# Row weights of a routed expert layer picked by GpSimd, row statistics and last normalisations two pairs a tile, additions to the result two by two

## The chip, the cores and the metric

The kernel runs on one core of one Trainium2 chip. The metric is the device time of one execution in microseconds; lower is better.

## The reference

For 2 x 1024 tokens of width 256 the result is `x + attention(xn) + experts(xn)`, with `xn` the rows of `x` normalised to mean 0 and variance 1.

```
xn = layernorm(x)
# "attention": a gated recurrence in logarithms
k = xn @ W_z.T + b_z
log_values = [g_log(h0) ; -softplus(-k) + g_log(xn @ W_h.T + b_h)]
a_star = pad(cumsum(-softplus(k), axis=-1))
log_h = a_star + cumlogsumexp(log_values - a_star, axis=1)
log_h = (log_h - log_h.mean()) / std(log_h)           # over everything
y = exp(log_h)[:, 1:, :] + xn
attention = layernorm(y) * ln_w + ln_b                # row by row
# experts: 8 experts, top 2 of each token, inner width 704
for e in range(8):
    experts += (silu(xn @ w1[e].T) * (xn @ w3[e].T)) @ w2[e].T * weight_of(e)
```

## The kernel before

**Setup.** The rows are normalised into `xn` (part of `xrow`, which holds for each token its 256 values and its two routing weights), transposed, and routed. The 4096 picks are sorted by expert into tiles of 128 rows, an expert's rows filling whole tiles; there are at least 33 tiles (`SURE`) and at most 39 (`NTILES`), and this input makes 36, numbered 0 to 35. `xrow` is stored to `xn_dram`, from which GpSimd gathers the rows of a tile with an indirect DMA (L390) into one of `DEEP` = 4 buffers `xg`.

**The tile loop.** It runs on all engines at once, each in its own fixed order, with semaphores between them. For tile j:

- TensorE: `up(j)` (L1296, 18 products: float32 values are split into a high and a low part, three products for one), the transpose of the rows of tile j+1 (L1265), a few instructions of the attention (`between`), `down(j-1)` (L1314, 18 products), and the transpose of the gated values, `h_tile(j)` (L1326).
- ScalarE: `silu(j)` (L595), the high part of the next rows (L572), `y_copy(j-1)` (L621: the down product times the row weights `wrow`, into a buffer of four, `ysb`), the high part of `hT` (L590), then its share of the next expert's weights (L604). In some tiles one attention step stands before or behind these, between two loads of an activation table (L696, L704).
- VectorE: `gate(j)` (L961), the low part of the next rows, `x_lo` (L952), `slot_weight(j+1)` (L1067: the weight of each of the 128 rows, one element a partition), `between(j)`, the low part of `hT`, `h_lo(j)` (L956), `after(j)`.
- GpSimd: `gather(j+4)` (L390), `scatter(j-1)` (L406: an indirect DMA that adds a tile's rows to the result), and `split_due(j)` (L424: the low parts of the next expert's weights, `raw` minus the high part).

**Weights.** Each expert's weights go through four pieces. While the first tile of an expert is at work two pieces of the next one are due, with its second tile one, with its third one. ScalarE makes a piece's high part, GpSimd its low part. `up` of an expert's first tile waits for three of its pieces, `down` for all four (`s_w`). The 28 pieces of L424 are those of experts 1 to 7, and on this input experts begin with tiles 0, 4, 9, 13, 18, 23, 28 and 32.

**Attention.** Its steps are put by hand into `between` and `after` of tiles 1 to 32: running maxima (tiles 3 to 9), scans (10 to 12), sums and statistics over all elements (13 to 18), the exponential (ScalarE, 19 and 20), then, for pairs m = 0 to 7 of 128-row blocks, `h_back(m)` on TensorE (L1354, four transposes) and `row_stats(m)` on VectorE in tile 20 + m, the square roots on ScalarE in tiles 24 and 28, `row_scales` in 25 and 29, and `last_norm(m)` (L1054, L1059) behind `h_lo` in tile 25 + m.

**Additions to the result.** `out` starts as a copy of x. Additions to it must not overlap, so each `scatter` waits until the one before has landed (`rows_added`: `s_st`), and until the attention's parts so far have landed (`s_ab`). `add_attention` (L413) adds a quarter of the attention rows, 512 KB, by a DMA from GpSimd's queue, with the same wait, before tiles 27, 29 and 31 and behind tile 32. Behind the loop come the tiles from 33 on, each in a nested condition (`tail`), then the last down product and a last scatter (L467) from `hst`.

Of the kernel before, what the change touches and what calls it, by code (L numbers as in the profile page):

```python
# [14 lines left out]
P = 128  # L15
B, T, D = 2, 1024, 256
# [36 lines left out]
def build_program(nc, x, small, w_main, w_tail, out, xn_dram):  # L53
# [5 lines left out]
    with ctx:  # L59
# [285 lines left out]
        def _(pool):  # L345
# [38 lines left out]
            def gather(j):  # L384

                if j >= DEEP:
# [4 lines left out]
                                        bass.IndirectOffsetOnAxis(gidx[:, j:j + 1], 0)).then_inc(s_gt[k], 16)  # L391

            def rows_added(j, parts):

                if j:
                    pool.wait_ge(s_st, 16 * j)
                if j == 0:
                    pool.wait_ge(s_fill, 16)
                if parts:
                    pool.wait_ge(s_ab, 16 * parts)  # L400
# [7 lines left out]

            def add_attention(j, m):

                pool.wait_ge(s_p2, 4 * m + 4)
                rows_added(j, m)
                pool.dma_start(out[4 * m * P:4 * (m + 1) * P, :].rearrange("(t p) d -> p t d", p=P),  # L413
                               xn[:, 4 * m:4 * m + 4, :], accum_op=ALU.add).then_inc(s_ab, 16)

# [10 lines left out]

            for j in range(DEEP + 1):
                gather(j)
            pool.wait_ge(s_idx, 1)
            pool.wait_ge(s_ctl, 1)  # L430
            split_due(0, 0)

            def tile(i, u, done=None, parts=PARTS_OF_H):

                j = LOOP * i + (1 + u)
                if j + DEEP < NTILES:
                    gather(j + DEEP)
                scatter(j - 1, parts)
                if done is None:
                    done = pool.value_load(plan[0:1, ds(j, 1)], min_val=0, max_val=PIECES * (E - 1))  # L440
                return split_due(done, j)

            added = 0
            for i in range(8):
                done = pool.value_load(plan[0:1, ds(LOOP * i + 1, 1)], min_val=0, max_val=PIECES * (E - 1))
                for u in range(LOOP):
                    j = LOOP * i + 1 + u
                    if j in (27, 29, 31):
                        add_attention(j - 1, added)
                        added += 1  # L450
                    done = tile(i, u, done, added)
            add_attention(SURE - 1, added)

# [20 lines left out]
        def _(act):  # L474
# [170 lines left out]

            def row_deviations(h):
                act.wait_ge(s_p1, 3 * (4 * h + 4))
                act.activation(std[:, 8 * h:8 * h + 8], mv[:, 8 * h:8 * h + 8, 1], ACT.Sqrt,
                               bias=eps[:, :]).then_inc(s_std3, 1)

# [32 lines left out]
            def roots(j):  # L683
                if j == 18:
                    deviation()
                else:
                    row_deviations((j - 24) // 4)

# [20 lines left out]
            for i in range(8):  # L709
                done = act.value_load(plan[0:1, ds(LOOP * i + 1, 1)], min_val=0, max_val=PIECES * (E - 1))  # L710
                for u in range(LOOP):
                    j = LOOP * i + 1 + u
                    if j in (3, 4, 5, 6, 7, 10, 11, 12, 13, 19, 20):
                        done = tile(i, u, done, "natural_log_exp_and_others", exp_log_first, exp_log_second)
                    elif j in (18, 24, 28):
                        done = tile(i, u, done, "sqrt_and_others", None, roots)
                    else:
                        done = tile(i, u, done)
# [11 lines left out]
        def _(dve):  # L730
# [315 lines left out]

            def row_scales(h):
                dve.wait_ge(s_std3, h + 1)
                dve.reciprocal(rstd[:, 8 * h:8 * h + 8], std[:, 8 * h:8 * h + 8]).then_inc(s_rs3, 1)
                dve.wait_ge(s_rs3, h + 1)  # L1050

# [10 lines left out]

            def slot_weight(j):

                k = j % DEEP
                dve.wait_ge(s_gt[k], 16 * (j // DEEP + 1))
                dve.scalar_tensor_tensor(wrow[:, j:j + 1], xg[:, k, D:D + 1], first_pick[:, j:j + 1],  # L1067
                                         xg[:, k, D + 1:D + 2], ALU.mult, ALU.max).then_inc(s_ws, 1)

            softplus(0)  # L1070
# [5 lines left out]
            x_lo(0, 0, xT0_ps)  # L1076
            slot_weight(0)
            softplus(2)
            add_cumsum(1)
            x_lo(1, 1, xT1_ps)  # L1080
            slot_weight(1)
            dve.wait_ge(s_u0b, 2)
# [10 lines left out]
            def between(j):  # L1093
# [12 lines left out]
                if 13 <= j <= 16:  # L1106
                    plus_max(j - 13)
                if 20 <= j <= 27:
                    row_stats(j - 20)

            def after(j):
# [32 lines left out]
                if j == 18:  # L1144
                    normaliser()
                if j in (25, 29):
                    row_scales((j - 25) // 4)
                if 25 <= j <= 32:
                    last_norm(j - 25)

            def tile(i, u, hooks=False):
# [3 lines left out]
                if not isinstance(j, int) or j < NTILES - 1:  # L1155
                    x_lo(j + 1, u % 2)
                    slot_weight(j + 1)
                if hooks:
# [12 lines left out]
        def _(pe):  # L1171
# [185 lines left out]
            def between(j):  # L1357
                if j in (4, 5, 6, 7):
                    half_cumsum(j // 2, 1 - j % 2)
                if 20 <= j <= 27:  # L1360
                    h_back(j - 20)

# [6 lines left out]
            def tile(i, u, hooks=False):  # L1369
# [12 lines left out]
                pe.reg_mov(r_e, expert(j + 1))  # L1382
                h_tile(j)

            for i in range(8):
# [45 lines left out]
```

## Time and profile before

| | |
|---|---|
| Median of 3 runs | 357.61 us (355.52 to 359.3) |
| The profiled execution's own time | 357.79 us |
| Its span, first to last instruction | 356.1 us |
| Mean granted TensorE clock, share of full speed | 0.969 |
| PE, DVE, ACT, POOL busy | 325.8, 260.8, 219.9, 206.4 us |

What lies outside the span is 1.7 us. Busy shares are means over stages with different limits: what a change is worth is read tile by tile. The names are PE for TensorE, DVE for VectorE, ACT for ScalarE, POOL for GpSimd. A GpSimd instruction's recorded start and end are rough.

### The profile page before, as it was taken

What the parts mean: (1) busy time and instruction counts of PE and PEld (TensorE: products, weight loads), DVE (VectorE), ACT (ScalarE), POOL (GpSimd) and SP (SyncE); (2) the same over time, 40 slices, a digit from 0 to 9 for tenths busy, and PEclk for the clock granted to TensorE, in tenths of its full rate; (3) what the DMA queues carried; (4) which work ended last, traced back from release to release, by engine and by line L of the source; (5) the groups of instructions that cost most, each with busy time, mean ns of one, the idle gap of its engine ahead of it and who ended that gap; (6) DMA issues with size and microseconds to landing.
All of it is one profiled execution on the core that took longest, in us unless ns stands there. A gap on an engine that the chain in (4) does not pass through costs nothing.

```text
span 356.1 us, 6682 instructions
## 1 busy us (share of the span) xinstructions
PE 325.8 (91%) x1964; PEld 273.9 (77%) x1964; DVE 260.8 (73%) x466; ACT 219.9 (62%) x328; POOL 206.4 (58%) x137
## 2 busy tenths in 40 slices
PE   8998999799999999999898999999999999979830
PEld 8883464588878898997787899889898988969730
DVE  5488787989996899889899842584589668763300
ACT  2547997455879974999854269934853485323400
POOL 4500023159968674989899728563885475945331
PEclk9999969989999999999999999999999999999985
DMA  7924912005444542354354434542463534354621
GB/s 263 426 120 137 293 52 59 15 11 150 122 82 115 142 101 32 80 129 129 44 144 109 102 38 115 142 101 33 84 181 89 75 45 76 47 76 49 98 38 15
DMA packets 19086, 37.00 MB, mean 104 GB/s; under 512 B 2272, under 2 KB 13536, under 8 KB 19008
## 3 DMA queue, kind: packets, MB, share of 16 engines
q0 software_dynamic: 9168, 11.97, 21.5%
q1 hardware_dynamic: 8496, 22.56, 20.4%
q10 hardware_dynamic: 1376, 1.85, 1.4%
q8 instruction: 29, 0.48, 0.6%
q14 instruction: 17, 0.14, 0.1%
HBM read 27.45 MB, written 11.03 MB: 108 GB/s over the span
## 4 chain that ended last, share of the span: by engine, by line
PE 54%; DVE 23%; ACT 8%; issue 8%; DMA 2%; ACTq 1%; POOL 1%; POOLq 0%; DVEq 0%
PE PS L1296 23%; PE PS L1314 11%; PE PS L1190 6%; PE PS L1326 5%; DVE wrow L1067 3%; DVE tmp L961 3%; PE PS L1176 2%; DMA out<-work,sidx 2%; DVE hT L956 2%; DVE U L985 2%; DVE A L998 1%; PE PS L1220 1%; DVE xrow L1054 1%; DVE xrow L1059 1%; PE PS L1265 1%
## 5 line engine op out<-in xcount | busy, mean ns | idle before, releaser
L1296 PE MATMUL PS<-wbuf,xT 128*128 128x512 f32 (+1 forms) x648 | 149.6, 384 | 4.9 <-issue 3.7
L1296 PEld LDWEIGHTS PS<-wbuf,xT 128*128 128x128 f32 x648 | 118.3, 190 | 29.4 <-issue 9.3
L424 POOL TENSOR_TENSOR wbuf<-raw,wbuf x28 | 81.4, 2924 | 23.1 <-ACT wbuf L604 21.4
L406 POOL DMA_INDIRECT out<-work,sidx x35 | 62.7, 1792 | 53.2 <-ACT work L621 20.1
L1314 PE MATMUL PS<-wbuf,hT 128*128 128x256 f32 x648 | 86.8, 288 | 0.0
L1314 PEld LDWEIGHTS PS<-wbuf,hT 128*128 128x128 f32 x648 | 79.3, 189 | 1.9 <-issue 1.9
L390 POOL DMA_INDIRECT work<-xn_dram,gidx x39 | 50.4, 1292 | 51.8 <-DVE gidx L892 36.1
L595 ACT ACTIVATE tmp<-PS 128x512 f32<-128x512 f32 x72 | 32.0, 460 | 41.6 <-PE PS L1296 41.3
L961 DVE TENSOR_TENSOR tmp<-tmp,PS 128x512 f32<-128x512 f32 x72 | 35.0, 516 | 29.4 <-ACT tmp L595 28.6
L956 DVE TENSOR_TENSOR hT<-PS,hT 128x768 fp32r<-128x768 f32 x36 | 34.2, 949 | 29.3 <-ACT hT L590 24.2
L621 ACT ACTIVATE work<-PS,wrow 128x256 f32<-128x256 f32 x35 | 16.4, 470 | 38.0 <-PE PS L1314 38.0
L1067 DVE SCALAR_TENSOR_TENSOR wrow<-work,first_pick 128x1 f32<-128x1 f32 x37 | 37.1, 1003 | 0.0
L1326 PE MATMUL PS<-ident,tmp 128*128 128x128 f32 x216 | 30.1, 275 | 5.7 <-DVE tmp L961 5.6
L590 ACT ACTIVATE hT<-PS 128x768 fp32r<-128x768 f32 x35 | 28.4, 810 | 10.4 <-PE PS L1326 10.4
L1190 PE MATMUL PS<-xnT_M,small_sb 128*128 128x512 f32 x64 | 32.3, 646 | 1.0 <-ACT tmp L525 1.0
L604 ACT ACTIVATE wbuf<-raw x28 | 30.4, 1110 | 4.0 <-issue 3.9
L1326 PEld LDWEIGHTS PS<-ident,tmp 128*128 128x128 f32 x216 | 24.0, 141 | 7.9 <-DVE tmp L961 6.9
L1190 PEld LDWEIGHTS PS<-xnT_M,small_sb 128*128 128x128 f32 x64 | 12.6, 208 | 14.1 <-issue 12.9
L704 ACT ACT_TABLE_LOAD x14 | 18.0, 1283 | 0.3
L696 ACT ACT_TABLE_LOAD x14 | 18.0, 1283 | 0.3
L952 DVE TENSOR_TENSOR xT<-PS,xT 128x256 fp32r<-128x256 f32 x37 | 15.5, 419 | 0.1
L572 ACT ACTIVATE xT<-PS 128x256 fp32r<-128x256 f32 x37 | 14.0, 381 | 1.7 <-PE PS L1265 1.7
(185 smaller groups left out, 350.7 us busy)
## 6 DMA issues: line engine op xcount, KB each, us to landing
raw<-w_main SPq DMA_DIRECT2D x24, 544.0 KB
raw<-w_main SPq DMA_DIRECT2D x8, 416.0 KB
xn_dram<-xrow SPq DMA_DIRECT2D x4, 516.0 KB, 7.2
out<-xrow POOLq DMA_DIRECT2D x4, 512.0 KB, 6.1
xrow<-x SPq DMA_DIRECT2D x4, 256.0 KB, 4.8
xrow<-x ACTq DMA_DIRECT2D x4, 256.0 KB, 5.4
small_sb<-small ACTq DMA_DIRECT2D x1, 768.0 KB, 7.9
work<-xn_dram,gidx POOLq DMA_INDIRECT x39
```

The source lines that it names most:

```text
L390: pool.indirect_dma_start(xg[:, k, :], None, xn_dram, bass.IndirectOffsetOnAxis(gidx[:, j:j + 1], 0)).then_inc(s_gt[k], 16)
L406: pool.indirect_dma_start(out, bass.IndirectOffsetOnAxis(sidx[:, j:j + 1], 0), ysb[:, j % DEEP, :], None, compute_op=ALU.add).then_inc(s_s ...
L424: pool.tensor_tensor(lo, raw[:, ds(part, WP)], hi.bitcast(fp32), ALU.subtract).then_inc(s_w, 1)
L595: act.activation(sls[n], w1_ps[n], ACT.Silu).then_inc(s_silu, 1)
L604: act.activation(wslot(p // PIECES + 1, 0, part), raw[:, ds(part, WP)], ACT.Copy).then_inc(s_hi, 1)
L956: dve.tensor_tensor(hT[:, 1, :], hT_ps, hT[:, 0, :].bitcast(fp32), ALU.subtract).then_inc(s_hlo, 1)
L961: dve.tensor_tensor(g_hs[n], sls[n], w3_ps[n], ALU.mult).then_inc(s_g, 1)
L1067: dve.scalar_tensor_tensor(wrow[:, j:j + 1], xg[:, k, D:D + 1], first_pick[:, j:j + 1], xg[:, k, D + 1:D + 2], ALU.mult, ALU.max).then_inc ...
L1190: ins = pe.matmul(PS[:, base + qo * CH:base + (qo + 1) * CH], wzh_sb[:, q, mat, qo * P:(qo + 1) * P], xnT[:, q, c * CH:(c + 1) * CH], star ...
L1296: ins = pe.matmul(PS[:, at:at + cols], xT[:, slot, xpart, q * P:(q + 1) * P], wbuf[:, w, wpart, q * 2 * F + at:q * 2 * F + at + cols], sta ...
L1314: ins = pe.matmul(y_ps, hT[:, hpart, c * P:(c + 1) * P], wbuf[:, w, wpart, W13 + c * D:W13 + (c + 1) * D], start=(c == 0 and hpart == 0 an ...
L1326: ins = pe.transpose(hT_ps[:, c * P:(c + 1) * P], g_h[:, a:a + P], ident[:, :])
```

## The change

Four things are moved, and no arithmetic is altered:

1. `slot_weight(j)` leaves VectorE for GpSimd, which makes it two tiles ahead: at the head of its tile j it does `slot_weight(j+2)`. There it is a `tensor_scalar` with two pointer scalars.
2. Row statistics: `h_back` and `row_stats` run two pairs a tile in tiles 20 to 23, where they ran one pair a tile in tiles 20 to 27. On TensorE the second `h_back` stands behind `h_tile(j)`.
3. `last_norm` runs two pairs a tile in tiles 25 to 28 (one before `h_lo`, one behind), where it ran one a tile in tiles 25 to 32. The square roots of all rows are made once, in tile 24, so that tile 28 loads no table.
4. `add_attention` adds two quarters in one go, before tiles 28 and 30.

In the order of the diff: GpSimd (to the second `add_attention`), ScalarE (`row_deviations` and its tiles), VectorE (`between`, `after`, `tile`), TensorE (`between`, `tile`).

```diff
+            def slot_weight(j):
+                k = j % DEEP
+                pool.wait_ge(s_gt[k], 16 * (j // DEEP + 1))
+                pool.tensor_scalar(wrow[:, j:j + 1], xg[:, k, D:D + 1], first_pick[:, j:j + 1],
+                                   xg[:, k, D + 1:D + 2], ALU.mult, ALU.max).then_inc(s_ws, 1)
...
-            def add_attention(j, m):
-                pool.wait_ge(s_p2, 4 * m + 4)
-                rows_added(j, m)
-                pool.dma_start(out[4 * m * P:4 * (m + 1) * P, :].rearrange("(t p) d -> p t d", p=P),
-                               xn[:, 4 * m:4 * m + 4, :], accum_op=ALU.add).then_inc(s_ab, 16)
+            def add_attention(j, first):
+                pool.wait_ge(s_p2, 4 * first + 8)
+                rows_added(j, first)
+                for m in (first, first + 1):
+                    pool.dma_start(out[4 * m * P:4 * (m + 1) * P, :].rearrange("(t p) d -> p t d", p=P),
+                                   xn[:, 4 * m:4 * m + 4, :], accum_op=ALU.add).then_inc(s_ab, 16)
...
-            for j in range(DEEP + 1):
+            for j in range(DEEP):
                 gather(j)
             pool.wait_ge(s_idx, 1)
+            slot_weight(0)
+            gather(DEEP)
+            slot_weight(1)
+            slot_weight(2)
...
                 j = LOOP * i + (1 + u)
+                if j + 2 < NTILES:
+                    slot_weight(j + 2)
                 if j + DEEP < NTILES:
                     gather(j + DEEP)
                 scatter(j - 1, parts)
...
-                    if j in (27, 29, 31):
+                    if j in (28, 30):
                         add_attention(j - 1, added)
-                        added += 1
+                        added += 2
                     done = tile(i, u, done, added)
-            add_attention(SURE - 1, added)
...
-            def row_deviations(h):
-                act.wait_ge(s_p1, 3 * (4 * h + 4))
+            def row_deviations():
+                act.wait_ge(s_p1, 3 * NT // 2)
...
-                    elif j in (18, 24, 28):
+                    elif j in (18, 24):
...
-                if 20 <= j <= 27:
-                    row_stats(j - 20)
+                if 20 <= j <= 23:
+                    row_stats(2 * (j - 20))
+                if j == 25:
+                    row_scales()
+                if 25 <= j <= 28:
+                    last_norm(2 * (j - 25))
...
-                if j in (25, 29):
-                    row_scales((j - 25) // 4)
-                if 25 <= j <= 32:
-                    last_norm(j - 25)
+                if 20 <= j <= 23:
+                    row_stats(2 * (j - 20) + 1)
+                if 25 <= j <= 28:
+                    last_norm(2 * (j - 25) + 1)
...
                     x_lo(j + 1, u % 2)
-                    slot_weight(j + 1)
...
-                if 20 <= j <= 27:
-                    h_back(j - 20)
+                if 20 <= j <= 23:
+                    h_back(2 * (j - 20))
...
                 h_tile(j)
+                if hooks and 20 <= j <= 23:
+                    h_back(2 * (j - 20) + 1)
```

## Rows read from the trace of the kernel before

**Rows 1.** The page, parts 1 and 4: busy time; the shares of the chain.
```profile
PE 325.8 (91%) x1964; PEld 273.9 (77%) x1964; DVE 260.8 (73%) x466; ACT 219.9 (62%) x328; POOL 206.4 (58%) x137
...
PE 54%; DVE 23%; ACT 8%; issue 8%; DMA 2%; ACTq 1%; POOL 1%; POOLq 0%; DVEq 0%
PE PS L1296 23%; PE PS L1314 11%; PE PS L1190 6%; PE PS L1326 5%; DVE wrow L1067 3%; DVE tmp L961 3%; PE PS L1176 2%; DMA out<-work,sidx 2%; DVE hT L956 2%; DVE U L985 2%; DVE A L998 1%; PE PS L1220 1%; DVE xrow L1054 1%; DVE xrow L1059 1%; PE PS L1265 1%
```

**Rows 2.** Lines L1067 and L424: ns min/median/max, first and last start.
```profile
L1067 DVE SCALAR_TENSOR_TENSOR wrow<-work,first_pick x37: 202/475/3761, 62.9 to 334.7; 128x1 f32<-128x1 f32 x37
...
L424 POOL TENSOR_TENSOR wbuf<-raw,wbuf x28: 2502/2750/4583, 75.1 to 308.1; - x28
```

**Rows 3.** Timeline of VectorE, tiles 3 and 32: start, duration, instruction.
```profile
92.72 2.95 DVE L1067 SCALAR_TENSOR_TENSOR wrow<-work,first_pick 128x1 f32<-128x1 f32 x1
95.60 2.34 DVE L968 TENSOR_TENSOR_SCAN xnT_M<-U,u 128x1024 f32<-128x1024 f32 x1
...
308.15 3.75 DVE L1054 SCALAR_TENSOR_TENSOR xrow<-xrow,mv,small_sb 128x256 f32<-128x256 f32 x2
...
316.10 0.87 DVE L1054 SCALAR_TENSOR_TENSOR xrow<-xrow,mv,small_sb 128x256 f32<-128x256 f32 x2
```

**Rows 4.** Timeline of GpSimd, tile 3 and from tile 26 to the end.
```profile
92.55 3.10 POOL L424 TENSOR_TENSOR wbuf<-raw,wbuf  x1
...
270.98 1.58 POOL L406 DMA_INDIRECT out<-work,sidx  x1 [1.30 <-ACT work L621]
275.44 1.40 POOL L413 DMA_DIRECT2D out<-xrow  x1 [2.88 <-DMA out<-work,sidx]
...
282.49 1.66 POOL L406 DMA_INDIRECT out<-work,sidx  x1 [4.26 <-DMA out<-xrow]
...
302.44 3.12 POOL L424 TENSOR_TENSOR wbuf<-raw,wbuf  x1
...
308.10 3.12 POOL L424 TENSOR_TENSOR wbuf<-raw,wbuf  x1
...
347.79 1.57 POOL L467 DMA_INDIRECT out<-hst,scol  x1 [2.67 <-DMA out<-work,sidx]
```

**Rows 5.** Windows: length; busy PE, PEld, DVE, ACT, POOL; clock, DMA share, GB/s.
```profile
70.55:102.79 32.24, 31.67 (x180) 27.11 (x181) 30.46 (x36) 21.00 (x31) 25.95 (x11) 0.95 0.38 92
154.48:203.11 48.63, 44.14 (x267) 38.23 (x267) 46.33 (x53) 32.25 (x48) 43.58 (x21) 1.00 0.49 115
133.65:140.50 6.85, 6.85 (x47) 6.26 (x46) 6.85 (x10) 2.49 (x6) 2.74 (x2) 1.00 0.27 42
217.15:233.58 16.43, 15.54 (x98) 13.52 (x97) 8.07 (x15) 15.63 (x21) 11.82 (x7) 1.00 0.54 135
240.90:248.18 7.28, 7.28 (x51) 6.69 (x49) 4.07 (x10) 2.49 (x6) 2.58 (x2) 1.00 0.27 41
262.77:270.86 8.09, 7.76 (x51) 6.75 (x50) 7.95 (x16) 3.82 (x8) 5.88 (x4) 1.00 0.54 131
285.01:299.28 14.27, 14.22 (x92) 12.59 (x90) 11.18 (x19) 9.57 (x16) 9.64 (x6) 1.00 0.41 58
```

**Rows 6.** Timeline of TensorE: up products of tiles 32, 33, 35; last down product.
```profile
306.15 4.11 PE L1296 MATMUL PS<-wbuf,xT 128*128 128x512 f32 x18
...
315.85 4.10 PE L1296 MATMUL PS<-wbuf,xT 128*128 128x512 f32 x18 [1.50 <-issue]
...
329.58 4.09 PE L1296 MATMUL PS<-wbuf,xT 128*128 128x512 f32 x18
...
339.65 2.38 PE L1314 MATMUL PS<-wbuf,hT 128*128 128x256 f32 x18
```

**Rows 7.** Group of GpSimd with one element a partition: busy us, mean ns.
```profile
L461 POOL COPY scol<-sidx 128x1 uint32 x1 | 0.2, 183 | 0.4 <-issue 0.4
```

**Rows 8.** DMA of one attention add: us to landing; window in its middle.
```profile
DMA to landing us min/median/max: 5.9/6.1/6.3
...
279.00:281.00 2.00, 2.00 (x10) 1.63 (x9) 1.72 (x3) 0.25 (x1) 0.00 (x0) 1.00 1.19 202
```

More of the change, by code:

```diff
@@ L644, in normal_exp @@
                 act.activation(Ag[:, g, :], Ag[:, g, :], ACT.Exp, scale=gs[:, 8:9], bias=gs[:, 9:10]).then_inc(s_hx, 1)
-            def row_deviations(h):
-                act.wait_ge(s_p1, 3 * (4 * h + 4))
-                act.activation(std[:, 8 * h:8 * h + 8], mv[:, 8 * h:8 * h + 8, 1], ACT.Sqrt,
-                               bias=eps[:, :]).then_inc(s_std3, 1)
+            def row_deviations():
+                act.wait_ge(s_p1, 3 * NT // 2)
+                act.activation(std[:, :], mv[:, :, 1], ACT.Sqrt, bias=eps[:, :]).then_inc(s_std3, 1)
             def exp_log_first(j):
@@ L686, in roots @@
                 else:
-                    row_deviations((j - 24) // 4)
+                    row_deviations()
             def tile(i, u, done=None, table=None, first=None, second=None):
@@ L1045, in row_stats, with row_scales @@
                 ins.then_inc(s_p1, 1)
[L1047 to L1050, printed above, removed]
+            def row_scales():
+                dve.wait_ge(s_std3, 1)
+                dve.reciprocal(rstd[:, :], std[:, :]).then_inc(s_rs3, 1)
+                dve.wait_ge(s_rs3, 1)
             def last_norm(m):
@@ L1061, in last_norm @@
                 ins.then_inc(s_p2, 1)
[L1063 to L1068, printed above, removed]
             softplus(0)
@@ L1076, in _ @@
             x_lo(0, 0, xT0_ps)
-            slot_weight(0)
             softplus(2)
@@ L1080, in _ @@
             x_lo(1, 1, xT1_ps)
-            slot_weight(1)
             dve.wait_ge(s_u0b, 2)
```

## The prediction

> **What bounds the kernel now.** I read the page first, then windows tile by tile, then the timelines of the tiles that are longer than the rest. TensorE is busy 91% of the span and holds 54% of the chain that ended last; VectorE holds 23% [rows 1]. A tile in which nothing waits takes 6.86 us, as tile 9 does, from 133.65 [rows 5]. Against it three kinds are longer. In tiles 1 to 4 and 12 to 17 (from 70.55 and from 154.48) VectorE is busy 30.46 of 32.24 us and 46.33 of 48.63: it paces them. In tiles 20 and 21 (from 217.15) ScalarE does, 15.63 of 16.43 us, with table loads and exponentials. Tile 23 (240.90 to 248.18) carries one `h_back`, 7.28 for 6.86, so four transposes cost 0.43 us [rows 5]. Single tiles stand out: 26 (8.09 us) and 32 (9.70, from 306.15 to 315.85) [rows 5, 6]. And the end isn't TensorE's: its last down product ends at 342.03, but the last scatter starts at 347.79, because GpSimd's additions, each waiting until the one before has landed, are behind [rows 4, 6].
>
> **Part 1, row weights.** On VectorE one takes 202 ns at least, 475 in the median and up to 3761 [rows 2], and the chain puts 3% of the span, some 11 us, on L1067 [rows 1]. The timeline shows what the long ones are: the one at 92.72 ends at 95.67, and GpSimd's piece of weights runs from 92.55 to 95.65 [rows 3, 4]. An instruction with two inputs in SBUF waits for GpSimd's to end. Who takes the wait over when the row weight is gone? The next VectorE instruction with two inputs in SBUF. In tile 3 that is the scan at 95.60 (`U`, `U`), which would start at 92.7 into the same piece [rows 3, 4]; likewise `less_n` in tiles 1 and 2, the scans in 8 to 10 and 12, `plus_max` in 13 to 16. In the other tiles the next step reads PSUM (4 to 7, 11, 20 to 27), but there VectorE doesn't pace. So the long waits are worth 0; only the undisturbed instruction is saved. Of its 0.20 us some 0.07 overlaps its neighbour (the scan starts at 95.60, the row weight ends at 95.67 [rows 3]), which leaves 0.13. Ten paced tiles and two in the setup: 12 x 0.13 = 1.6 us gained. The bounds are 0 and the chain's 11.
>
> The Trainium skill, "SBUF — State Buffer", section "Who interferes with whom", says that a VectorE instruction with two SBUF inputs and a GpSimd one that reads SBUF exclude each other, and whoever issues first has the pair for the whole instruction. The trace agrees in tile 3. By that rule the order decides, so that VectorE, 0.13 us earlier, could now win where it lost: rival 1.
>
> On GpSimd the new instruction has no row. The nearest is the copy of one element a partition, 0.18 us with 0.4 idle before it [rows 7]; the far bound is one kept waiting by a VectorE scan, 2.34 us [rows 3]. I take 0.3, near the copy. Queued behind it are `gather`, `scatter` and `split_due`, and TensorE and ScalarE wait for those. But GpSimd is busy 58% [rows 1], and the weight is used two tiles later: it costs nothing until tile 27, and after that one of them lies on GpSimd's chain (part 4). The waits of 2.34 belong to tiles up to 12.
>
> **Part 2, statistics.** `h_back` costs 0.43 us where TensorE paces. Tiles 20 and 21 are ScalarE's: 16.43 us against 2 x 7.28 leave 1.9 us of waiting, in which their second ones hide. Tiles 22 and 23 gain one (+0.86), tiles 24, 25 and 27 lose theirs (-1.29); in 26 VectorE's wait for a piece of weights fills what comes free. Sum -0.4. VectorE has room for a second `row_stats`: it is busy 4.07 of 7.28 us in tile 23 [rows 5], one of them included.
>
> **Part 3, last normalisations.** An undisturbed pair of instructions takes 0.87 us, so a `last_norm` 1.75 [rows 3]. Two of them beside some 2.4 us of the usual work (tile 23's 4.07 less its statistics, about 1.7) make 5.9 of 6.86: tiles 25 to 28 hold. In tile 32 a pair takes 3.75 us, because the piece from 308.10 to 311.22 runs [rows 3, 4], and the tile becomes 9.70 us, 2.84 too long. Of that 1.5 stands as "issue" before `up(33)` [rows 6], where the nested tail begins, and stays; 1.3 goes, as no normalisation is left in tile 32. So does 0.55 in tiles 29 and 30 (14.27 us from 285.01 [rows 5]), which is ScalarE behind a table load and VectorE behind a piece. Sum -1.9.
>
> **Part 4, additions, and what hangs on them.** Let S be the start of `up(27)`, 270.86 before, where tile 26's window ends [rows 5]. From one add of attention to the scatter behind it GpSimd needs 282.49 - 275.44 = 7.05 us, 6.1 of them to landing [rows 4, 8]. Two in a row have no row. In the middle of one, data flow at 202 GB/s [rows 8], so the second's 0.51 MB adds 2.6 us at least; if it is as slow as the first it adds 4.7 (6.1 less the issue, 1.40 [rows 4]). That is 8.7 to 10.8 to landing; I take the middle, 9.8, and 10.6 to the scatter.
>
> GpSimd's new course, TensorE taking 6.86 a tile: `scatter(26)` at S + 7.8; it has landed 4.46 later (270.98 to 275.44 [rows 4]); the first two adds at S + 12.3; `scatter(27)` at S + 22.9; after 1.4, two pieces of 2.6 (2502 ns at least, median 2750 [rows 2]) to S + 29.5; row weight, gather, `scatter(28)` at S + 31.2; 1.1 later expert 7's third piece, to S + 34.9. `up(32)`, the first of expert 7, is due at S + 5 x 6.86 = S + 34.3. Before, the piece ended at 305.56 and `up(32)` began at 306.15 [rows 4, 6]: 0.6 us to spare; now it is late, and with the start-up behind the wait TensorE loses 1.3. The second two adds go at S + 35.4, `scatter(29)` at S + 46.0, and the fourth piece ends at S + 49.8; before, it ended at 311.22 = S + 40.4 [rows 4]. `down(32)` is due at S + 35.6 + 6.86 + 1.5 + 4.1 = S + 48.1; TensorE loses 2.0. Two new waits, +3.3.
>
> The end: from the start of `up(35)`, 329.58 [rows 6], to the end of the span at 356.1 it is 26.5 us. No add of attention stands between scatters any more after S + 46; five scatters at 4.5 us bring `scatter(34)` to S + 68.5, and its rows, ready 7 us behind `up(35)` at S + 59.7, have hardly waited. The last row copy follows 12.6 us behind `up(35)` (its last down product ends 12.45 behind it [rows 6]), the last scatter 1.4 later, and the end 8.3 behind that (347.79 to 356.1 [rows 4]): 22.3 us, -4.2.
>
> **The sum**: -1.6 - 0.4 - 1.9 + 3.3 - 4.2 = -4.8. It is made against the profiled execution's own 357.79, of which 1.7 lies outside the span: 353.0. That execution stands 0.2 above the median of the runs shown, which I neglect.
>
> **Rivals.** (1) Row weights' waits are real gains, partly because VectorE now gets in first, and the weights of expert 7 are in time. For it: some 11 us of the chain [rows 1]. Against it: tile 3's next instruction. A quarter of them beyond my 1.6 gives -2.3, no new wait at tile 32 -3.3: 347.4. (2) Nothing to speak of: a pair of adds shares the queue with a gather and takes 2.4 more than I say. Each us of that counts twice for the fourth piece: +4.5, 357.5. (3) Slower: the second add gains nothing from the first, so that pair and gather take 2 x 7.05 + 1 = 15.1 to the scatter, 4.5 over mine. The fourth piece is 9 later, `down(32)` waits for it, 362.0. It turns slower than before when a pair takes more than 2.4 us over my 10.6. (4) The change doesn't do what it says, row weights on GpSimd coming late behind scans. With two tiles of lead it is next to nothing, and would look like rival 2.
>
> The Trainium skill, "GPSIMD Engine Reference", section "Performance versus the Vector engine", has GpSimd about twice as slow at elementwise work: an estimate from that page is 0.4 us for VectorE's 0.2. The one on the chain would cost 0.1 more, the sum 353.1; no run here shows it yet.
>
> **Chances.** Forecast 0.50, rival 1 0.22, rival 2 0.17, rival 3 0.08, rival 4 0.03. Within 1%, 3.6 us, is about what a measurement of this kernel can't tell from no change: 354.0 to 361.2. The forecast's own spread, 350 to 356 by the bounds of a pair and of the 1.6, puts a third of it there. Faster: 0.33 + 0.22 and a little = 0.57; same 0.36; slower 0.07. The range of 8 in 10 reaches from 346.5, just beyond rival 1, to 358.0, just beyond rival 2.
>
> **What would show it.** VectorE's instruction behind `x_lo` in tiles 3, 12 and 15 should be the long one now, up to 2.9 us over its usual time. Tiles 29 and 30 should take 6.86. The scatter behind a pair should start 10.6 us behind its first add. `up(32)` and `down(32)` should wait for L424. The last scatter should start within 1.5 us of the last row copy. I am wrong if those scans are short (rival 1), if a pair takes 13 us or more (rival 3), or if TensorE waits for statistics in tiles 22 to 25.

## The result and the profile after

The changed kernel takes 364.35 us in the median of four runs (363.06 to 366.3), the kernel before 356.89 beside it on the same chip (355.52 to 359.3). The ratio is 1.0193, with a 95% interval from 1.0139 to 1.0246: slower, by 1.4 to 2.5%, where 353.0 us and a gain of 4.8 were forecast, and beyond the range. The profiled execution took 365.17 us, with a span of 363.4 against 356.1; the changed parts are read from it.

From the page, part 1, then the GpSimd row of part 2 (busy tenths in 40 slices of 9.1 us), and two groups of part 5:

```profile
PE 331.9 (91%) x1964; PEld 278.9 (77%) x1964; DVE 252.3 (69%) x428; ACT 217.3 (60%) x325; POOL 237.8 (65%) x175
...
POOL 4500024169999999999899937864699346948731
...
L397 POOL TENSOR_SCALAR wrow<-work,first_pick 128x1 f32<-128x1 f32 x38 | 54.4, 1433 | 0.1
...
L997 DVE TENSOR_TENSOR_SCAN U<-tmp,U 128x1024 f32<-128x1024 f32 x4 | 15.7, 3918 | 0.0
```

VectorE has lost 8.5 us of busy time against [rows 1], GpSimd has gained 31.4. Its 65% is a mean: from about 80 to 210 us nearly every slice is 9 tenths full. The 38 row weights alone take 54.4 us on it. The view of their source line:

```profile
L397 POOL TENSOR_SCALAR wrow<-work,first_pick x38: 353/1002/3043, 57.7 to 345.8; 128x1 f32<-128x1 f32 x38
```

An undisturbed one takes 0.35 us, the median is 1.00 and the longest 3.04. On VectorE the three numbers were 0.20, 0.48 and 3.76 [rows 2].

**Where the time went**, from the starts of `up(j)` in the two traces (tile j is the time from the start of `up(j)` to that of `up(j+1)`, us; the setup took 0.56 longer, which experiment 1, with the same setup, doesn't repeat):

| stretch | before | after | difference |
|---|---|---|---|
| tile 8 | 6.86 | 8.21 | +1.35 |
| tile 12 | 7.78 | 10.32 | +2.54 |
| tile 15 | 7.50 | 10.01 | +2.51 |
| start of `up(20)`, everything ahead included | 217.15 | 224.09 | +6.9 |
| tiles 20 and 21 | 16.43 | 17.25 | +0.8 |
| tiles 22, 23; 24, 25 | 14.59; 14.59 | 15.48; 13.72 | +0.9; -0.9 |
| tile 26 | 8.09 | 9.13 | +1.0 |
| tile 27 | 7.30 | 8.41 | +1.1 |
| tiles 29 and 30 | 14.27 | 13.73 | -0.5 |
| tile 31 | 6.87 | 7.70 | +0.8 |
| tile 32 | 9.70 | 7.75 | -2.0 |
| tile 33 | 6.87 | 10.80 | +3.9 |
| `up(35)` to the end | 26.5 | 21.7 | -4.8 |

Most of the loss lies ahead of tile 20, where of the whole change only the row weights have been moved. Up to `up(27)` the sum is +8.8, behind it -1.4. From the start of `up(0)` to that of `up(20)` (153.7 us before, 160.1 now) VectorE is busy 137.4 us for 135.8, GpSimd 134.5 for 113.9: VectorE's waits have hardly grown in sum, but they stand in other places.

**Ahead of tile 20.** GpSimd's timeline, tiles 11 to 14 of after (start, duration, instruction):

```profile
157.03 0.94 POOL L397 TENSOR_SCALAR wrow<-work,first_pick 128x1 f32<-128x1 f32 x1
...
160.55 3.09 POOL L432 TENSOR_TENSOR wbuf<-raw,wbuf  x1
163.07 2.89 POOL L397 TENSOR_SCALAR wrow<-work,first_pick 128x1 f32<-128x1 f32 x1
...
170.06 3.10 POOL L432 TENSOR_TENSOR wbuf<-raw,wbuf  x1
172.56 2.92 POOL L397 TENSOR_SCALAR wrow<-work,first_pick 128x1 f32<-128x1 f32 x1
```

and VectorE's in the same stretch:

```profile
160.04 5.76 DVE L997 TENSOR_TENSOR_SCAN U<-tmp,U 128x1024 f32<-128x1024 f32 x1
...
166.90 2.27 DVE L997 TENSOR_TENSOR_SCAN U<-tmp,U 128x1024 f32<-128x1024 f32 x1
...
169.95 5.36 DVE L997 TENSOR_TENSOR_SCAN U<-tmp,U 128x1024 f32<-128x1024 f32 x1
...
183.76 5.62 DVE L1003 TENSOR_TENSOR U<-U,xnT_M 128x1024 f32<-128x1024 f32 x1
```

The scan at 160.04 takes 5.76 us, an undisturbed one 2.27 (166.90). The piece of weights runs until 163.64, and the scan ends 2.16 us after that: it waited for the piece. (The piece's recorded start is 0.5 us behind the scan's; GpSimd's starts are rough, so the reading goes by the ends.) GpSimd's next instruction is the row weight at 163.07. It ends at 165.96, just behind the scan's end at 165.80: it waited for the scan, and what stands behind it on GpSimd waited too. The same happens at 170.06 and 172.56. The two pieces start 9.51 us apart.

The same two pieces in the kernel before, and VectorE beside them:

```profile
154.42 3.10 POOL L424 TENSOR_TENSOR wbuf<-raw,wbuf  x1
...
161.48 3.10 POOL L424 TENSOR_TENSOR wbuf<-raw,wbuf  x1
164.74 2.87 POOL L390 DMA_INDIRECT work<-xn_dram,gidx  x1 [0.16 <-issue]
```

```profile
152.58 0.95 DVE L961 TENSOR_TENSOR tmp<-tmp,PS 128x512 f32<-128x512 f32 x2 [2.17 <-ACT tmp L595]
...
153.78 3.76 DVE L1067 SCALAR_TENSOR_TENSOR wrow<-work,first_pick 128x1 f32<-128x1 f32 x1
...
158.34 2.27 DVE L985 TENSOR_TENSOR_SCAN U<-tmp,U 128x1024 f32<-128x1024 f32 x1
```

Here they start 7.06 us apart. The first one starts 3.9 us ahead of the scan at 158.34 and is over at 157.52, so that this scan is undisturbed, and VectorE's row weight takes the wait in a tile in which VectorE has just waited 2.17 us for ScalarE. At 164.74 the gather is held up behind a piece, so such stops of GpSimd were there before. From 75 to 205 us the gathers took 27.0 us (18 of them) before and take 17.4 (16) now, beside 37.1 for 16 row weights: the row weight takes over the gather's stops and adds longer ones.

How late GpSimd is can be read from each `scatter(j)`, from the end of the copy that makes its rows ready to its start. For j = 8 to 11 this was 0.8, 5.4, 3.2 and 4.4 us before and is 6.2, 8.8, 9.0 and 10.8 now.

### The profile page after: what moved, and what is told of

Same layout as the page of the kernel before. It is cut to its first block and busy times, and to the rows that moved or that the text cites. A ratio compares the mean times of both kernels' runs of the same rounds, so it can differ in the third digit from the quotient of the medians.

```text
span 363.4 us, 6677 instructions
## 1 busy us (share of the span) xinstructions
PE 331.9 (91%) x1964; PEld 278.9 (77%) x1964; DVE 252.3 (69%) x428; ACT 217.3 (60%) x325; POOL 237.8 (65%) x175
## 5 line engine op out<-in xcount | busy, mean ns | idle before, releaser
L1302 PE MATMUL PS<-wbuf,xT 128*128 128x512 f32 (+1 forms) x648 | 154.0, 393 | 4.3 <-issue 2.9
L1302 PEld LDWEIGHTS PS<-wbuf,xT 128*128 128x128 f32 x648 | 121.7, 195 | 30.0 <-issue 8.8
L413 POOL DMA_INDIRECT out<-work,sidx x35 | 66.3, 1895 | 42.7 <-ACT work L634 22.3
L1320 PE MATMUL PS<-wbuf,hT 128*128 128x256 f32 x648 | 88.5, 291 | 2.5 <-POOL wbuf L432 2.2
L432 POOL TENSOR_TENSOR wbuf<-raw,wbuf x28 | 80.2, 2937 | 15.7 <-ACT wbuf L617 15.7
L1320 PEld LDWEIGHTS PS<-wbuf,hT 128*128 128x128 f32 x648 | 80.8, 192 | 4.8 <-issue 4.8
L390 POOL DMA_INDIRECT work<-xn_dram,gidx x39 | 43.4, 1114 | 47.0 <-DVE gidx L904 36.3
L397 POOL TENSOR_SCALAR wrow<-work,first_pick 128x1 f32<-128x1 f32 x38 | 54.4, 1433 | 0.1
L997 DVE TENSOR_TENSOR_SCAN U<-tmp,U 128x1024 f32<-128x1024 f32 x4 | 15.7, 3918 | 0.0
```

Of the source, the lines that this page charges most:

```text
L390: pool.indirect_dma_start(xg[:, k, :], None, xn_dram, bass.IndirectOffsetOnAxis(gidx[:, j:j + 1], 0)).then_inc(s_gt[k], 16)
L397: pool.tensor_scalar(wrow[:, j:j + 1], xg[:, k, D:D + 1], first_pick[:, j:j + 1], xg[:, k, D + 1:D + 2], ALU.mult, ALU.max).then_inc(s_ws, 1)
L413: pool.indirect_dma_start(out, bass.IndirectOffsetOnAxis(sidx[:, j:j + 1], 0), ysb[:, j % DEEP, :], None, compute_op=ALU.add).then_inc(s_s ...
L432: pool.tensor_tensor(lo, raw[:, ds(part, WP)], hi.bitcast(fp32), ALU.subtract).then_inc(s_w, 1)
L1302: ins = pe.matmul(PS[:, at:at + cols], xT[:, slot, xpart, q * P:(q + 1) * P], wbuf[:, w, wpart, q * 2 * F + at:q * 2 * F + at + cols], sta ...
L1320: ins = pe.matmul(y_ps, hT[:, hpart, c * P:(c + 1) * P], wbuf[:, w, wpart, W13 + c * D:W13 + (c + 1) * D], start=(c == 0 and hpart == 0 an ...
```

## The experiments

Ratios are to the kernel before, run on the same chip beside each group of four. "Up(20)" is the start of `up(20)` in the trace.

**Experiment 1: part 1 alone.** The diff is the change's own, `slot_weight` with its three calls in the setup and the one in GpSimd's `tile`; the rest is the kernel before.

> The kernel before with part 1 alone: row weights by GpSimd two tiles ahead; statistics, normalisations and additions as before. Theory G (GpSimd late): a row weight costs GpSimd 1 to 3 us where VectorE works on two SBUF inputs, puts it some 4 us further behind in tiles 1 to 15, and shifts the weight pieces into VectorE's scans: 5 to 8 us slower than before (1.015 to 1.022), the loss in tiles 8, 12 and 15. Theory P (pairs): the two pairs a tile of statistics and normalisations and the paired additions are what costs: this kernel is then within 2 us of before.

Measured: 362.88 us, 1.0191 [1.0146, 1.0236]; `up(20)` at 223.32, 6.2 later than before; tiles 8, 12 and 15 take 8.24, 10.34 and 9.96. The row weights take 355 ns at least, 968 in the median, 3026 at most. That is theory G's case: part 1 by itself costs as much as the whole change.

**Experiment 2: parts 2 and 3 alone** (statistics and normalisations two pairs a tile; additions of attention one by one as before).

```
-                if 20 <= j <= 27:
-                    row_stats(j - 20)
+                if 20 <= j <= 23:
+                    row_stats(2 * (j - 20))
...
-                if 25 <= j <= 32:
-                    last_norm(j - 25)
+                if 20 <= j <= 23:
+                    row_stats(2 * (j - 20) + 1)
+                if 25 <= j <= 28:
+                    last_norm(2 * (j - 25) + 1)
```

> Parts 2 and 3 alone: statistics two pairs a tile, last normalisations two pairs a tile, row weights on VectorE, the four additions one by one in their old places. Theory G: tiles 20 to 23 cost about what 24 to 27 give back, tiles 29 to 32 are shorter, 0 to 3 us faster than before (0.992 to 1.0). Theory P: 2 to 4 us slower, lost in tiles 20 to 27.

Measured: 357.82 us, 1.0048 [1.0025, 1.0071], so a small loss. Tile 32 falls from 9.70 to 6.85 us, but tiles 20 and 21 rise from 8.27 and 8.16 to 10.50 and 9.30, and 29 to 7.96. TensorE at the end of tile 20, and VectorE there:

```profile
224.02 0.88 PE L1329 MATMUL PS<-ident,tmp 128*128 128x128 f32 x6
226.67 0.63 PE L1357 MATMUL PS<-ident,A 128*128 128x128 f32 x4 [1.78 <-DVE xrow L1036]
227.52 4.78 PE L1299 MATMUL PS<-wbuf,xT 128*128 128x512 f32 x13 [0.22 <-issue]
```

```profile
224.48 1.45 DVE L1066 SCALAR_TENSOR_TENSOR wrow<-work,first_pick 128x1 f32<-128x1 f32 x1
225.85 0.68 DVE L1036 TENSOR_TENSOR xrow<-PS,xrow 128x512 f32<-128x512 f32 x1
```

`h_back(1)` stands ahead of `up(21)` and writes where `h_back(0)` wrote, so it waits until the add of `row_stats(0)` (L1036) has read that. The add stands behind `x_lo` and the row weight, which at 224.48 waits 1.2 us for a piece of GpSimd. Tile 20 pays for that wait with the 1.78 us, and tile 21 once more: its granted clock is 0.82, where the kernel before has 1.00 in both tiles. At the end nothing is gained: the last down product starts at 339.98 (339.65 before [rows 6]), the last scatter at 347.92 (347.79 before [rows 4]), and it waits until the one before has landed. GpSimd's additions set the end.

**Experiment 3: parts 2 to 4**, that is the change without part 1.

> The changed kernel with part 1 undone: row weights back on VectorE, parts 2, 3 and 4 kept. Theory G: the 7 us lost ahead of tile 20 come back, and the end gains as in the changed kernel: 2 to 4 us faster than before (0.989 to 0.995). Theory P: as slow as the changed kernel, 5 us or more over before.

Measured: 358.63 us, 1.0084 [1.0056, 1.0112]. `up(20)` is where it was (217.14). Tile 20 takes 10.50 us, and the wait of `down(32)` is there without any row weight on GpSimd:

```profile
317.07 4.11 PE L1299 MATMUL PS<-wbuf,xT 128*128 128x512 f32 x18 [0.53 <-issue]
...
324.07 3.67 PE L1317 MATMUL PS<-wbuf,hT 128*128 128x256 f32 x18 [2.68 <-POOL wbuf L425]
```

Tile 33 takes 11.08 us for 6.87. I had expected these parts to gain; they lose 3.0 us. Together with experiment 1 (+6.8) that is 9.8, where the whole change loses 6.9: the row weight on GpSimd takes away 2.5 us of what tiles 20 and 21 cost here (10.50 + 9.29 against 9.14 + 8.11).

**Experiment 4: the row weight on VectorE with one input.** Both its factors are scalars of a row, so one of them can be the instruction's pointer operand.

```
-                dve.scalar_tensor_tensor(wrow[:, j:j + 1], xg[:, k, D:D + 1], first_pick[:, j:j + 1],
-                                         xg[:, k, D + 1:D + 2], ALU.mult, ALU.max)
+                dve.tensor_scalar(wrow[:, j:j + 1], xg[:, k, D:D + 1], first_pick[:, j:j + 1],
+                                  xg[:, k, D + 1:D + 2], ALU.mult, ALU.max)
```

> The kernel before with the row weight on VectorE as a tensor_scalar: one tensor input and two pointer scalars, the form that the change uses on GpSimd. If the second tensor input is what makes it wait for GpSimd, no row weight takes over 0.5 us any more. Theory I (the wait is inherited by the next VectorE instruction with two SBUF inputs): the time is within 2 us of before, and the scans and subtractions of tiles 3, 12 and 15 become 2 to 3 us longer. Theory R (the waits were real losses, as the chain has them): 4 to 8 us faster.

Measured: 356.09 us, 1.0001 [0.9978, 1.0023]. The source line of its row weights:

```profile
L1067 DVE TENSOR_SCALAR wrow<-work,first_pick x37: 256/265/268, 63.0 to 337.0; 128x1 f32<-128x1 f32 x37
```

No row weight waits any more, and the kernel is no faster. So 3% of the chain on L1067 [rows 1] was worth nothing: the next instruction with two inputs in SBUF waits in its place, in tiles 3 and 12 the scan right behind it (undisturbed 2.34 and 2.28 us). Rival 1 falls.

```profile
92.96 4.90 DVE L968 TENSOR_TENSOR_SCAN xnT_M<-U,u 128x1024 f32<-128x1024 f32 x1
...
161.66 5.37 DVE L985 TENSOR_TENSOR_SCAN U<-tmp,U 128x1024 f32<-128x1024 f32 x1
```

**Experiment 5: GpSimd late, and nothing else.** The kernel before, with four fills of 128 x 512 elements in each of GpSimd's tiles 1 to 15, each waited for.

```
+            idle = sb("idle", [P, 512])
...
+                if j <= 15:
+                    for _ in range(4):
+                        step(pool.memset(idle[:, :], 0.0))
```

> The kernel before (row weights on VectorE), with four memsets of a spare buffer of 128 x 512 elements on GpSimd at the head of its tiles 1 to 15, each waited for: some 2.5 us a tile in which GpSimd is late but reads nothing in SBUF. It computes the same. Theory G1 (what costs is that GpSimd, and with it the weight pieces, comes some 2 to 4 us later): tiles 8, 12 and 15 grow as in the run with GpSimd's row weights, 4 to 7 us in all (1.011 to 1.02). Theory G2 (what costs is that the row weight on GpSimd itself reads SBUF and stands between VectorE and its second input): within 1.5 us of before.

Measured: 370.45 us, 1.0355 [1.0304, 1.0405]; a fill takes 0.53 us, 1.10 at most; `up(20)` at 231.80, 14.7 later. Up to tile 15 the scatters start 6 to 15 us behind their rows. From 154.48 to 203.11 GpSimd is busy 44.83 us for 43.58 [rows 5], VectorE 42.06 for 46.33. Lateness is enough for such a loss, although no instruction of VectorE gained an opponent beyond the fills' own writes, and it costs more than I had expected: at least 2.1 us a tile on GpSimd become nearly 1 us a tile on TensorE. It is a stronger dose than the change's, and not all of it goes the same way: `up(13)`, an expert's first tile, waits 3.3 us for its piece by the semaphore, which in the change no tile ahead of 20 does.

**Experiment 6: part 1, the row weight behind the scatter** and ahead of the pieces.

```
-                if j + 2 < NTILES:
-                    slot_weight(j + 2)
                 if j + DEEP < NTILES:
                     gather(j + DEEP)
                 scatter(j - 1, parts)
+                if j + 2 < NTILES:
+                    slot_weight(j + 2)
```

> Part 1 alone as in the first experiment, but GpSimd makes the row weight behind its scatter and ahead of the weight pieces, where it does not directly follow a piece. Theory G1: the row weights that took 3 us, because a waiting VectorE instruction went first when a piece ended, take under 1.5 in most tiles; GpSimd is less late, and 2 to 5 of the 6 us come back (1.004 to 1.013). If the place is all the same: 1.019 as there.

Measured: 359.82 us, 1.0064 [1.0036, 1.0092]. `up(20)` starts at 218.73, 1.6 later than before instead of 6.2. From 75 to 205 us the row weights take 23.1 us (16 of them) for 37.0 in experiment 1, but the gathers, which again stand behind the pieces, take 29.1 (17) for 17.6 (16): what follows on a piece waits for VectorE, whichever it is. GpSimd is busy 112.4 us of the 125 from 75 to 200, in experiment 1 117.9, in the kernel before 104.2, and the pieces come again nearly as early as before (144.4, 155.4 and 164.5 for 143.7, 154.4 and 161.5; 152.0, 160.5 and 170.1 in the change). So the row weight's place in GpSimd's order, by which the pieces come a few us earlier or later, decides most of part 1's loss. The 1.6 us left are a balance: tile 15 still takes 10.59 us for 7.50, while tiles 12, 13 and 16 are 0.6, 1.0 and 0.8 shorter than before.

**Experiment 7: parts 2 to 4, pieces ahead of the scatter** in GpSimd's tiles 28 to 31.

```
+                first = 28 <= j <= 31
+                if not first:
+                    scatter(j - 1, parts)
...
+                done = split_due(done, j)
+                if first:
+                    scatter(j - 1, parts)
+                return done
```

> Parts 2 to 4 as in the third experiment (row weights on VectorE), with GpSimd making the weight pieces ahead of the scatter in tiles 28 to 31, so that they do not stand behind the landing of the two additions. If the waits of up(32) and down(32) are the price of the pairs: both go, the fourth piece ends 8 us or more earlier, and TensorE gains 3.5 to 5 us over the third experiment, of which the end keeps 2 to 5: 0.992 to 1.002 of before. If they are not: 1.008 as there.

Measured: 354.63 us, 0.9923 [0.9892, 0.9955]. GpSimd around the second pair:

```profile
307.15 2.71 POOL L414 DMA_DIRECT2D out<-xrow  x2 [3.11 <-issue]
...
311.24 2.59 POOL L425 TENSOR_TENSOR wbuf<-raw,wbuf  x1
316.92 1.65 POOL L406 DMA_INDIRECT out<-work,sidx  x1 [3.09 <-issue]
```

The last piece ends at 313.83, inside the time in which the pair lands (9.77 us from add to scatter), for 323.62 in experiment 3. Both waits are gone, tile 33 takes 6.87 us, and 1.0084 becomes 0.9923.

**Experiment 8: parts 2 to 4 with the row weight of experiment 4.**

> Parts 2 to 4 as in the third experiment, with the row weight on VectorE in the form with one tensor input, which does not wait for GpSimd. Theory H (tiles 20 and 21 grew by 2.2 and 1.1 us because the second h_back stands ahead of the next up and waits for row_stats, which stood behind a row weight that waited for GpSimd's piece): tile 20 falls from 10.5 to some 9.1 us, tile 21 to about 8.2: 1.5 to 2.5 us less than the third experiment (1.002 to 1.005). If the statistics themselves are too much for tile 20: it stays at 10.5.

Measured: 356.02 us, 0.9955 [0.993, 0.9979], a lower ratio than expected; the span is 1.7 us shorter than in experiment 3, as expected. Tile 20 takes 9.32 us for 10.50, tile 21 8.12 for 9.29, 26 8.10; tile 33 keeps its wait (11.14). So the row weight's wait was behind 2.35 us of what tiles 20 and 21 cost in experiments 2 and 3: 1.18 by itself, as TensorE waits 0.59 us at the end of tile 20 for 1.78, and 1.17 through the clock in tile 21 (1.00 here, 0.82 there). 1.05 us stay in tile 20, and in experiment 9 too.

**Experiment 9: parts 2 to 4 with both mends** (those of experiments 4 and 7).

> Parts 2 to 4 with both of the mends: row weight on VectorE with one tensor input, and the pieces ahead of the scatter in tiles 28 to 31. Theory: the two act in different places (tiles 20 and 21; 31 to 33) and add up: 0.9923 for the one, and some 1.5 to 2.5 us for the other: 0.985 to 0.989, span about 351. If they share a wait: 0.992.

Measured: 351.2 us, 0.9836 [0.9787, 0.9886], so the two mends add up. Tile 20 takes 9.32 us, 32 7.50, 33 6.87; the last scatter starts at 341.81.

**Experiment 10: the whole change, mended as in experiments 6 and 7**, the row weight staying on GpSimd.

> The changed kernel whole, row weights on GpSimd, with two things moved: the row weight behind the scatter (behind the gather in tiles 28 to 31), and the pieces ahead of the scatter in tiles 28 to 31. Theory G1: ahead of tile 20 it costs the 1.6 us that were left in the sixth experiment, the rest acts as in the ninth: 0.992 to 0.998. If GpSimd's row weights cost something wherever they stand: over 1.005.

Measured: 354.85 us, 0.9938 [0.9908, 0.9968]; `up(20)` at 218.55, tile 15 10.62, tile 33 6.85. Against experiment 9 the row weight on GpSimd costs 3.65 us even in its better place.

**Experiment 11: experiment 9 with the pieces ahead of the scatter in every tile up to 31** (`first = j <= 31`).

> As the ninth, but the pieces stand ahead of the scatter in all tiles up to 31, so that they come up to 3 us earlier where GpSimd is behind. Theory G1 in the other direction: pieces that come earlier end before VectorE's scans and subtractions in tiles 12 to 17, which shrink: 1 to 4 us faster than the ninth. If it is only lateness that hurts and the usual place is early enough, or the earlier place meets others: within 1 us of the ninth, or slower.

Measured: 350.56 us, 0.9812 [0.9774, 0.9851], the fastest of all. Against experiment 9 tiles 13, 4 and 17 fall (8.05 for 9.66 us; 8.58 for 9.47; 7.26), tile 15 rises (9.34 for 7.41). The two intervals overlap, and the difference isn't shown.

**Experiment 12: both mends without any part of the change** (`first = 27 <= j <= 32`, since the adds stand elsewhere).

> The kernel before with the two mends and none of the change's parts: row weight with one tensor input, pieces ahead of the scatter in tiles 27 to 32, additions one by one. Theory: tile 32 still holds a normalisation and the last addition still stands before the last scatters, so the end is not shortened: 0.996 to 1.001. If the mends are the whole gain of the ninth: as fast as the ninth.

Measured: 360.56 us, 1.0103 [1.0061, 1.0145]: slower than before, where I had expected no change. TensorE starts `up(35)` at 327.31, 2.3 earlier than in [rows 6], but GpSimd ends so:

```profile
329.73 1.38 POOL L413 DMA_DIRECT2D out<-xrow  x1 [2.68 <-issue]
...
336.53 1.64 POOL L406 DMA_INDIRECT out<-work,sidx  x1 [4.04 <-issue]
...
344.87 1.55 POOL L406 DMA_INDIRECT out<-work,sidx  x1 [2.50 <-DMA out<-work,sidx]
...
349.73 1.57 POOL L472 DMA_INDIRECT out<-hst,scol  x1 [2.73 <-DMA out<-work,sidx]
```

From `up(35)` to the end of the span it is 30.6 us, in the kernel before 26.5, in experiment 9 23.9. With scatters later and four adds one by one, the last of them at 329.73, each scatter up to the last waits until the one before has landed. So the gain of experiment 9 isn't the mends' alone: with nearly the same mends (the pieces go first in tiles 27 to 32 here, in 28 to 31 there), parts 2 to 4 are worth 9.4 us, 6.7 of them in this tail. Which of the two mends makes this kernel slower than before no run separates; experiment 4, with the first alone, was not slower.

## Why the prediction was wrong, point by point

By its own steps the sum was 353.0 - 357.8 = -4.8, and the profiled execution came to +7.4. The stretch ahead of `up(27)` was given -1.6 and took +8.8 (0.56 of it in the setup); the stretch behind it was given -3.2 and took -1.4. Of the miss of 12.2 us, 8.5 lie ahead of `up(20)` and belong to one step, 0.8 in tiles 20 and 21, 1.0 in tile 26 and 1.8 behind `up(27)`.

**The step that failed: "On GpSimd ... I take 0.3 ... it costs nothing until tile 27".** Three things were wrong in it. The size: 0.35 us is the least, 1.43 the mean, 3.04 the longest, beyond the far bound of 2.34; from 75 to 205 us 16 row weights took 37.1 us, 2.3 each. The cover: "GpSimd is busy 58%" is a mean over the span, and in just the tiles that VectorE paces [rows 5] has it busy 25.95 us of 32.24 (1 to 4) and 43.58 of 48.63 (12 to 17). Six row weights of 0.3 us would have fitted into the 5.05 us free in tiles 12 to 17; at 2.3 each they take 13.9 and make it late. The reader: I asked when the weight itself is used. It never was late. Late were the pieces and scatters that stand behind it on GpSimd, and ahead of tile 20 nobody waited for them by a semaphore; a later piece meets another instruction of VectorE, a scan or a sum of attention on which TensorE's next tile hangs, in place of an instruction that waited anyway. Experiment 1 shows that part 1 makes the loss (+6.2 us at `up(20)`), experiment 5 that lateness of GpSimd makes such a loss without any row weight on it (+14.7, 3.3 of it a wait for a piece), experiment 6 that 4.6 of the 6.2 go when another order brings the pieces back to nearly their old times. Why a given piece meets a given scan is chance of the schedule; no formula for it was found, and tile 17 came out 0.95 us shorter.

**What takes over the waits on VectorE: right as long as GpSimd isn't late.** "So the long waits are worth 0" was tested by experiment 4, 1.0001, and there the scans behind the row weight in tiles 3 and 12 are the long ones, as I had said. In the changed kernel only tile 15 shows that sign (L1003 at 183.76, behind `x_lo`). In tiles 3 and 12 the scan behind `x_lo` takes 2.33 and 2.27 us, undisturbed, and others wait, because the pieces come later; the scans of L997 take 3.92 us in the mean for 2.27 undisturbed. The 1.6 us for the instruction itself can't be seen beside the rest; experiment 4 keeps an instruction of 0.26 us and says nothing of it. The rule of the Trainium skill that I leaned on, "SBUF — State Buffer", section "Who interferes with whom", holds in both directions: the scan at 160.04 waited for a piece, the row weight at 163.07 for the scan. I had used one direction alone. The Trainium skill's other rule, "GPSIMD Engine Reference", section "Performance versus the Vector engine", gave an estimate of 0.4 us; 0.35 was measured for a row weight that nothing disturbs, and the mean is four times that.

**Part 2: half right.** Tiles 22 to 25 went as summed (+0.89 and -0.87). Tiles 20 and 21, where the second `h_back` was to hide in 1.9 us of ScalarE's waiting, cost 0.8 in the change and 3.4 without part 1 (experiment 2): `h_back(1)` waits for VectorE's first add, not for ScalarE, and part 2 put it ahead of `up(21)`. Experiment 8 divides this into 2.35 us of a row weight's wait, half of it by the clock behind it, and 1.05 of the move itself. In tile 26 I had VectorE's wait for a piece fill what comes free; it took 1.04 us more than that, as the second normalisation (L1071 at 274.03, 3.96 us) meets a piece that now runs from 274.20, and TensorE waits 1.67 us for the gate behind it.

**Part 3: right but for tile 26.** Tiles 29 and 30 take 6.86 and 6.87, -0.54 for -0.55. Tile 32 gained 2.0 where I had 1.3. That "tiles 25 to 28 hold" is so for 25 and 28 (6.87 and 6.86 us); in 26 a normalisation meets a piece (above), and 27, where I had 6.87, takes 8.41 by the clock behind that wait (below).

**Part 4: the mechanism right, two sizes off.** The first add to the scatter behind a pair is 9.79 and 9.70 us for my 10.6. GpSimd and TensorE at the end of after:

```profile
293.46 2.71 POOL L421 DMA_DIRECT2D out<-xrow  x2 [2.88 <-DMA out<-work,sidx]
...
303.25 1.62 POOL L413 DMA_INDIRECT out<-work,sidx  x1 [5.36 <-issue]
...
316.25 2.77 POOL L421 DMA_DIRECT2D out<-xrow  x2 [0.28 <-issue]
...
325.95 1.62 POOL L413 DMA_INDIRECT out<-work,sidx  x1 [5.21 <-issue]
327.16 2.95 POOL L432 TENSOR_TENSOR wbuf<-raw,wbuf  x1
...
349.52 1.59 POOL L413 DMA_INDIRECT out<-work,sidx  x1 [3.19 <-ACT work L634]
...
355.09 1.59 POOL L480 DMA_INDIRECT out<-hst,scol  x1 [3.70 <-ACT hst L737]
```

```profile
316.35 4.09 PE L1302 MATMUL PS<-wbuf,xT 128*128 128x512 f32 x18 [0.60 <-POOL wbuf L432]
...
330.57 3.91 PE L1320 MATMUL PS<-wbuf,hT 128*128 128x256 f32 x18 [2.15 <-POOL wbuf L432]
```

`up(32)` and `down(32)` wait for L432, as said. They cost 0.8 and 3.9 us for 1.3 and 2.0. The second one's wait is 2.15 in itself; of the rest 1.5 is TensorE's clock behind it (below), for which the sum had no term. The last two scatters wait for ScalarE's copies and not for a landing, where the last one waited for a landing in [rows 4]: the end is 21.7 us behind `up(35)` for my 22.3, a gain of 4.8. Experiment 12 shows from the other side what the adds one by one cost.

**Rivals.** Rival 1 was refuted by experiment 4, and the weights of expert 7 weren't in time either; rivals 2 and 3 by the pair's 9.7 us. Rival 4 named GpSimd's lateness, but for the row weights' readers, and it got 0.03. The slower case I priced was the wrong one.

## What to carry to other kernels

When an instruction is moved to an engine, take that engine's busy share in the stretch where it lands, and ask of everything queued behind it what it will now run beside; a semaphore's slack doesn't cover it where two engines exclude each other on a memory. An instruction on one element a partition is cheap only until it stands between two large ones of the other engine, so don't queue it directly behind a large one; here the best place was VectorE, with one tensor input (experiment 9 against 7 and 10). A chain of additions that wait for each other's landing is shortened by issuing two transfers in a row, provided that what the next stage needs (here weights) goes ahead of the waiting instruction and not behind it (parts 2 and 3 alone have the ratio 1.0048; with the pairs behind which the weights stand 1.0084, with the weights ahead 0.9923).

## What the runs showed of the hardware

**The order in which the two engines get through.** When VectorE's scan waits for a piece on GpSimd, it runs as soon as the piece ends, and GpSimd's next instruction, although it was due at once, waits for the whole scan (163.64, 165.80 and 165.96 above). VectorE's instruction with one input and two pointer operands in SBUF doesn't wait at all: 268 ns at most in 37, with the same pieces around it.

**Two adds of 512 KB in a row** take 9.70 to 9.79 us from the first's issue to the next scatter, one takes 7.05: the second adds 2.7 us, near the 2.6 that 202 GB/s gives for 0.51 MB and far from a whole 4.7.

**TensorE's clock behind a wait.** After four of the waits the next products run slower. Windows by tile of after (length; busy PE, PEld, DVE, ACT, POOL; clock, DMA share, GB/s), tiles 15, 16, 26, 27 and 33:

```profile
184.35:194.36 10.01, 7.56 (x44) 6.38 (x45) 9.97 (x9) 3.57 (x7) 9.53 (x6) 1.00 0.61 146
194.36:202.78 8.42, 8.42 (x44) 7.46 (x45) 8.36 (x9) 3.40 (x6) 7.95 (x6) 0.80 0.49 104
270.52:279.65 9.13, 7.33 (x47) 6.31 (x46) 9.06 (x14) 3.81 (x8) 8.18 (x8) 1.00 0.51 117
279.65:288.06 8.41, 8.41 (x44) 7.45 (x45) 6.76 (x15) 2.29 (x5) 3.26 (x3) 0.80 0.35 80
...
324.09:334.89 10.80, 8.64 (x44) 7.84 (x45) 2.34 (x4) 1.78 (x5) 8.29 (x7) 0.84 0.31 50
```

In tile 26 TensorE is idle for 1.8 us, 1.67 of them in one wait, and in tile 27, where it is busy all the time, the granted clock is 0.80, a mix of its levels of 1.2 and 2.4 GHz: its 18 up products take 5.65 us for 4.11, and the tile 8.41 for 7.30 before, when it had an `h_back` of 0.43 in it. Tile 16 is the same behind tile 15, and tile 13 (0.84) behind tile 12. In tile 33 the fall comes behind the wait of `down(32)`: its products take 3.91 us for 2.38. In the kernel before all four tiles had 1.00. Where TensorE paces, as in 27 and 33, the wait of about 2 us costs some 1.5 us more than itself; in tiles 13 and 16 VectorE paces, and they took 9.51 and 8.42 us for 9.24 and 8.49. Such a wait doesn't always lower the clock: in the kernel before TensorE waits 1.74 us at the end of tile 13, and 0.88 and 1.50 us in tile 32, and tiles 14 and 33 have 1.00. What decides it these runs don't show.
